# A graph block on one core: the last group's deviations by square root and reciprocal, the group in front of it written out by GpSimd

## What is computed

```python
def _layernorm(x, axis=-1, eps=1e-05):
    m = jnp.mean(x, axis=axis, keepdims=True)
    v = jnp.var(x, axis=axis, keepdims=True)
    return (x - m) / jnp.sqrt(v + eps)

# attention: per graph h = x (128x128), four score kinds, adj picks one of them
e_k = leaky_relu(einsum('bid,bjd->bij', h * a_k[:, 0], h))
alpha = softmax(where(adj == k + 1, e_k, ...))          # NEG_INF elsewhere
x = _layernorm(x + einsum('bij,bjd->bid', alpha, h))
# relational convolution, one relation for each value of adj, per direction
vals = (h[:, :, None, :] + b) * sigmoid(g[:, :, None, :] + bg)   # h = x W^T, g = h Wg^T
out = relu(sum over directions of einsum('bnmr,bmrd->bnd', onehot, vals))
x = _layernorm(x + out)
```

## Time and profile before

| | before |
|---|---|
| time, median of 3 runs | 107.75 us (107.31 to 108.19) |
| time of the profiled execution | 107.57 us |
| its span, first to last instruction | 105.8 us |
| TensorE busy | 97.1 us (92%), granted clock 0.994 |
| VectorE busy | 93.5 us (88%) |
| ScalarE busy | 89.3 us (84%) |
| GpSimd busy | 76.3 us (72%) |
| share of 16 DMA engines of the queue with all loads and stores | 52.5% |

### The profile page before, as it was taken

The page is one execution under the profiler, slowest core; times in us unless marked ns, Lnnn a source line. Parts: engine busy times, 40 slices in busy tenths (PEclk is TensorE's granted clock), DMA queues, the critical chain, the costliest instruction groups (busy, mean ns, idle before and its releaser), DMA issues.

```text
span 105.8 us, 2755 instructions
## 1 busy us (share of the span) xinstructions
PE 97.1 (92%) x682; PEld 88.6 (84%) x682; DVE 93.5 (88%) x375; ACT 89.3 (84%) x224; POOL 76.3 (72%) x139
## 2 busy tenths in 40 slices
PE   6998969999999999999999999999999998999700
PEld 6975948999999999999999999999999997888400
DVE  0169999989999999899999999999999989789970
ACT  5149998989998898999999998996999868896750
POOL 5015787598627979996989997989998981757660
PEclk9999999999999999999999999999999999999997
DMA  1999999997416258499990303011203030330355
GB/s 43 329 364 371 367 351 371 347 348 240 152 53 223 81 133 266 107 300 296 320 257 18 99 3 95 10 49 50 82 20 99 6 105 0 99 99 0 99 149 158
DMA packets 22530, 17.36 MB, mean 164 GB/s; under 512 B 1265, under 2 KB 18418, under 8 KB 22514
## 3 DMA queue, kind: packets, MB, share of 16 engines
q1 hardware_dynamic: 22370, 17.18, 52.5%
q10 hardware_dynamic: 144, 0.00, 0.1%
HBM read 12.98 MB, written 4.19 MB: 162 GB/s over the span
## 4 chain that ended last, share of the span: by engine, by line
PE 76%; SPq 6%; DMA 5%; issue 4%; DVE 4%; ACT 2%; POOL 1%; DVEq 0%
PE p_hg L1252 25%; PE p_o L1223 13%; PE p_ag L1272 12%; PE p_e L1193 9%; PE p_yt L1239 6%; PE p_ut L1212 5%; DMA inputs<-adj_rows 5%; PE p_e L1196 3%; SPq L712 2%; SPq L713 2%; DVE res L1063 1%; ACT absent L900 1%; DVE vals L1093 1%; POOL late_rs L882 1%; SPq L719 1%
## 5 line engine op out<-in xcount | busy, mean ns | idle before, releaser
L1252 PE MATMUL p_hg<-w_both,y_t 128*128 128x256 f32 x128 | 30.5, 380 | 0.0
L1252 PEld LDWEIGHTS p_hg<-w_both,y_t 128*128 128x128 f32 x128 | 23.1, 190 | 2.7 <-ACT y_t L989 0.2
L934 ACT ACTIVATE prob<-nscore,nmax 128x128 f32<-128x128 f32 x64 | 20.3, 395 | 1.2 <-DVE nmax L1048 1.2
L854 POOL TENSOR_TENSOR rs<-rs,minus_half 128x8 f32<-128x8 f32 x12 | 20.2, 1681 | 0.0
L1063 DVE SCALAR_TENSOR_TENSOR res<-p_o,rz,inputs 128x128 f32<-128x128 f32 x64 | 18.0, 345 | 0.8 <-DVE rz L1055 0.3
L1223 PE MATMUL p_o<-inputs,prob_t 128*128 128x129 f32 x128 | 17.0, 275 | 0.0
L1223 PEld LDWEIGHTS p_o<-inputs,prob_t 128*128 128x128 f32 x128 | 16.0, 191 | 0.6 <-issue 0.2
L1272 PE MATMUL p_ag<-vals,mask 128*128 128x128 f32 x116 | 15.9, 278 | 0.4 <-DVE vals L1093 0.3
L1272 PEld LDWEIGHTS p_ag<-vals,mask 128*128 128x128 f32 x116 | 14.3, 191 | 1.1 <-issue 1.0
L998 ACT ACTIVATE th<-p_hg 128x256 f32<-128x256 f32 x32 | 11.6, 379 | 3.8 <-PE p_hg L1252 3.7
L1193 PE MATMUL p_e<-inputs,xat 128*128 128x128 f32 x104 | 14.0, 278 | 0.0
(11 more groups left out here) (101 smaller groups left out, 176.6 us busy)
## 6 DMA issues: line engine op xcount, KB each, us to landing
inputs<-x_t SPq DMA_DIRECT2D x16, 256.0 KB, 5.3
inputs<-adj_rows SPq DMA_DIRECT2D x16, 256.0 KB, 5.6
inputs<-x SPq DMA_DIRECT2D x16, 256.0 KB, 6.0
out<-out_s SPq DMA_DIRECT2D x14, 256.0 KB, 2.3
out<-xat SPq DMA_DIRECT2D x4, 128.0 KB, 2.1
w_rows<-w SPq DMA_DIRECT2D x1, 128.0 KB, 3.4
wg_s<-wg_t SPq DMA_DIRECT2D x1, 128.0 KB, 3.6
w_rows<-w SPq DMA_DIRECT2D x1, 64.0 KB, 5.1
```

Source lines behind the costliest of these rows:

```text
L854: nc.gpsimd.tensor_tensor(rs[:, k, 1], rs[:, k, 0], minus_half[:], ALU.pow).then_inc(rstd1_done, 1)
L934: nc.scalar.activation(prob[:, k, i], nscore[:, k, i], ACT.Exp, scale=-1.0, bias=nmax[:, k, i:i + 1]).then_inc(exp_done, 1)
L1252: last = nc.tensor.matmul(p_hg[:, 2 * h + i], y_t[:, g % 2, part(g, h)][:, i], w_both[:], start=True, stop=True)
```

## The change

The last group's reciprocal deviations no longer come from GpSimd. ScalarE takes the square root of the variance plus epsilon (new stages std_h0:15 and std_h1:15, into last_std), and VectorE takes the reciprocal (rstd_h0:15, rstd_h1:15, into late_rs). ScalarE's square root needs another function table: a stage load_roots:15 runs a dummy square root so that the table is loaded there, and a dummy exponential behind ScalarE's last stage loads the old table again. Group 14's four outputs, by VectorE and ScalarE before, are all written by GpSimd (finish_p_h0:14, finish_p_h1:14, one instruction a graph), which also makes the negated means (late_minus). Its two half stores wait for GpSimd's semaphore alone. Columns of epsilon (eps_col) are set by one more memset at the start.

```diff
@@ -38,7 +38,7 @@
-OUT_BY = ["pppp"] * 10 + ["vvss"] * 3 + ["ssss"] + ["vsvs", "vsvv"]
+OUT_BY = ["pppp"] * 10 + ["vvss"] * 3 + ["ssss"] + ["pppp", "vsvv"]
...
@@ -65,7 +65,7 @@
-        tanhs_h0:15 tanhs_h1:15 finish_s:13 finish_s_h0:14 finish_s_h1:14 finish_s_h0:15
+        tanhs_h0:15 tanhs_h1:15 load_roots:15 finish_s:13 std_h0:15 std_h1:15 finish_s_h0:15
...
@@ -725,9 +737,12 @@
                 sp.dma_start(wg_s[:, FWD:], wg_t[FWD:].rearrange("k f e -> f k e")).then_inc(others_loaded, 16)
 
             def store_half(g, h):
-                for by, made_by in (("v", out_by_v), ("s", out_by_s)):
-                    if by in OUT_BY[g][half(h)]:
-                        sp.wait_ge(made_by, out_made(by, g - 1) + OUT_BY[g][0:2 * h + 2].count(by))
+                if g == SPLIT[0]:
+                    sp.wait_ge(late_out_by_p, 2 * h + 2)
+                else:
+                    for by, made_by in (("v", out_by_v), ("s", out_by_s)):
+                        if by in OUT_BY[g][half(h)]:
+                            sp.wait_ge(made_by, out_made(by, g - 1) + OUT_BY[g][0:2 * h + 2].count(by))
                 sp.dma_start(out_v[:, graphs(g)][:, half(h)], late_out(g)[:, half(h)]).then_inc(stored[g % 2], 16)
 
             def store(g):
...
@@ -754,6 +769,7 @@
+            nc.gpsimd.memset(eps_col[:], EPS).then_inc(const_done, 1)
...
@@ -878,12 +894,23 @@
                 pool.wait_ge(st2_done, START[g] // 2 + h + 1)
                 nc.gpsimd.tensor_scalar(late_rs[:, k, 0, half(h)], late_st[:, k, half(h), 2], 1.0 / P, EPS, ALU.mult, ALU.add)\
                     .then_inc(var2_done, 1)
+                nc.gpsimd.tensor_scalar(late_minus[:, half(h)], late_st[:, k, half(h), 1], -1.0, None, ALU.mult)\
+                    .then_inc(late_minus_done, 1)
                 pool.wait_ge(var2_done, normed_half(g, h))
                 nc.gpsimd.tensor_tensor(late_rs[:, k, 1, half(h)], late_rs[:, k, 0, half(h)], minus_half[:, half(h)],
                                         ALU.pow).then_inc(rstd2_done, 1)
 
+            def finish_p_half(g, h):
+                k = late(g)
+                pool.wait_ge(rstd2_done, normed_half(g, h))
+                pool.wait_ge(late_minus_done, h + 1)
+                for i in range(2 * h, 2 * h + 2):
+                    nc.gpsimd.tensor_scalar(late_out(g)[:, i], late_res(g)[:, i], late_minus[:, i:i + 1],
+                                            late_rs[:, k, 1, i:i + 1], ALU.add, ALU.mult).then_inc(late_out_by_p, 1)
+
             run("gpsimd", {"weigh_p": weigh, "prepare_w": prepare_w, "norm1": norm1, "y_p": y_p, "norm2": norm2, "norm2_h0": lambda g: norm2_half(g, 0),
                            "norm2_h1": lambda g: norm2_half(g, 1),
+                           "finish_p_h0": lambda g: finish_p_half(g, 0), "finish_p_h1": lambda g: finish_p_half(g, 1),
                            "norms": both_norms, "finish_p": finish_p})
             general_pool(pool)
 
...
@@ -964,17 +991,25 @@
                     nc.scalar.activation(out_s[:, k, i], res2[:, k, i], ACT.Identity, scale=rs2[:, k, 1, i:i + 1],
                                          bias=shift2[:, k, i:i + 1]).then_inc(out_by_s, 1)
 
+            def load_roots(g):
+                act.wait_ge(const_done, 8)
+                nc.scalar.activation(table_loader[:], ones_col[:], ACT.Sqrt).then_inc(roots_loaded, 1)
+
+            def std_half(g, h):
+                act.wait_ge(st2_done, START[g] // 2 + h + 1)
+                nc.scalar.activation(last_std[:, half(h)], late_st[:, late(g), half(h), 2], ACT.Sqrt, scale=1.0 / P,
+                                     bias=eps_col[:]).then_inc(last_std_done, 1)
+
             def finish_s_half(g, h):
-                k, shifts = late(g), out_made("s", g) - out_made("s", SPLIT[0] - 1)
-                if h == 0 and "s" in OUT_BY[g][half(1)]:
-                    shifts -= 1
-                act.wait_ge(late_shift_done, shifts)
-                act.wait_ge(rstd2_done, normed_half(g, h))
+                k = late(g)
+                act.wait_ge(late_shift_done, OUT_BY[g][0:2 * h + 2].count("s"))
+                act.wait_ge(last_rstd_done, h + 1)
                 act.wait_ge(r2_done, summed(g, h))
                 for i in range(2 * h, 2 * h + 2):
                     if OUT_BY[g][i] == "s":
-                        nc.scalar.activation(late_out(g)[:, i], late_res(g)[:, i], ACT.Identity, scale=late_rs[:, k, 1, i:i + 1],
-                                             bias=late_shift[:, k, i:i + 1]).then_inc(out_by_s, 1)
+                        nc.scalar.activation(late_out(g)[:, i], late_res(g)[:, i], ACT.Identity,
+                                             scale=late_rs[:, k, 1, i:i + 1], bias=late_shift[:, k, i:i + 1])\
+                            .then_inc(out_by_s, 1)
 
             def evac_weights(g):
                 act.wait_ge(w_pe, 1)
...
@@ -1006,8 +1041,10 @@
-                           "finish_s_h1": lambda g: finish_s_half(g, 1),
+                           "finish_s_h1": lambda g: finish_s_half(g, 1), "load_roots": load_roots,
+                           "std_h0": lambda g: std_half(g, 0), "std_h1": lambda g: std_half(g, 1),
+            nc.scalar.activation(table_loader[:], minus_half[:, 0:1], ACT.Exp).then_inc(table_restored, 1)
...
@@ -1112,9 +1149,13 @@
                 nc.vector.scalar_tensor_tensor(out=late_res(g)[:, half(h)], in0=sums_bank(g, h), scalar=0.0,
                                                in1=y[:, g % 4, half(h)], op0=ALU.max, op1=ALU.add).then_inc(r2_done, 1)
 
+            def rstd_half(g, h):
+                dve.wait_ge(last_std_done, h + 1)
+                nc.vector.reciprocal(late_rs[:, late(g), 1, half(h)], last_std[:, half(h)]).then_inc(last_rstd_done, 1)
+
             def finish_half(g, h):
                 k = late(g)
-                dve.wait_ge(rstd2_done, normed_half(g, h))
+                dve.wait_ge(last_rstd_done, h + 1)
                 dve.wait_ge(st2_done, START[g] // 2 + h + 1)
                 for i in range(2 * h, 2 * h + 2):
                     if OUT_BY[g][i] == "s":
```

More of the change, by code:

```diff
@@ L82 @@
         stats2:13 values_h1:14 residual2_h0:14 stats2_h0:14 finish_v:12 residual2_h1:14 values_h0:15 stats2_h1:14
-        values_h1:15 residual2_h0:15 stats2_h0:15 residual2_h1:15 finish_v_h0:14 stats2_h1:15 finish_v_h1:14
-        finish_v_h0:15 finish_v_h1:15
+        values_h1:15 residual2_h0:15 stats2_h0:15 residual2_h1:15 stats2_h1:15 rstd_h0:15 finish_v_h0:15 rstd_h1:15 finish_v_h1:15
         """,
@@ L90 @@
         finish_p:7 norms:12 finish_p:8 norms:13 finish_p:9 norms:14 norms:15 norm2:12 norm2:13 norm2_h0:14 norm2_h1:14
-        norm2_h0:15 norm2_h1:15
+        finish_p_h0:14 finish_p_h1:14
         """,
@@ L181, in program @@
         late_rs = sb("late_rs", [P, 2, 2, G])
+        last_std = sb("last_std", [P, G])
+        late_minus = sb("late_minus", [P, G])
+        eps_col = sb("eps_col", [P, 1])
         late_shift = sb("late_shift", [P, 2, G])
@@ L238, in program @@
         late_shift_done = sem("late_shift_done")
+        late_out_by_p = sem("late_out_by_p")
+        late_minus_done = sem("late_minus_done")
+        roots_loaded = sem("roots_loaded")
+        last_std_done = sem("last_std_done")
+        last_rstd_done = sem("last_rstd_done")
+        table_restored = sem("table_restored")
         tanh_done = [sem(f"tanh_done{h}") for h in range(2)]
@@ L574, in groups_of @@
             by = stage[-1]
+            if stage[:-3] in ("norm2", "finish_p"):
+                return SPLIT[:1]
+            if stage == "load_roots" or stage[:-3] in ("std", "rstd", "finish_v"):
+                return SPLIT[1:]
             if stage[:-3] == "finish_s":
@@ L1160, in _ @@
                            "stats2_h0": lambda g: stats2_half(g, 0), "stats2_h1": lambda g: stats2_half(g, 1),
+                           "rstd_h0": lambda g: rstd_half(g, 0), "rstd_h1": lambda g: rstd_half(g, 1),
                            "finish_v_h0": lambda g: finish_half(g, 0), "finish_v_h1": lambda g: finish_half(g, 1)})
```

## The result

The changed kernel takes 108.73 us (median of 8 runs, 108.48 to 109.35) against 107.34 us of the kernel before in the same comparison (8 runs, 107.26 to 108.19). The ratio is 1.0103, with a 95% interval of 1.0071 to 1.0134: slower by about 1.1 us by the ratio (the two medians lie 1.39 us apart; the next paragraphs say why). Forecast was 108.2 in 107.6 to 109.0, so the time lies in the range and the sign is right, but the loss is twice the +0.55 of the sum.

The account below looks back on a forecast made before the run. TensorE was busy 92%, but the end was taken as set by the in-order sync queue behind late store 13: +0.55 us gives 108.12 from 107.57 or 108.30 from the 107.75 median; forecast 108.2 us, range 107.6 to 109.0.

Parts of the forecast that it names:

- The load in front of group 13: ScalarE, after the last tanh: load 1.28 us and dummy 0.20 make group 13 1.50 us late, store 13 issued at 101.84.
- That rival (0.13): ScalarE's mid-stream table switch costs more than the load, about 1.28 us again for emptying and refilling: 109.5 us; chance 0.13.
- The path of the deviations: Group 15: ScalarE roots from 101.82, 0.28 us each, then VectorE reciprocals and outputs to 103.44; covered by 0.28 us.
- the +0.2 of the prediction: Group 15's deviation chain, ending at 103.44, would set the end if store 13 were not in the way: +0.2 us.
- Group 14 on GpSimd: GpSimd's four outputs of 0.45 us: halves ready at 101.05 and 101.94, queue wants them at 102.31 and 102.78; no cost.
- The queue behind store 13: Sync queue: five stores back to back from 101.84, last issue at 103.72, landing 2.02 later, end at 105.74 by issue rate.
- Four more steps of 0.47: Sync queue, four half stores behind store 13: issues 0.47 us apart put the last issue at 103.72.
- the 0.11 that I had put on top of the issue sum: Kernel's end: landing taken at 105.85, between the issue sum of 105.74 and the slower data sum of 106.04.
- The stall: Sync queue: the unexplained 0.4 us wait before the issue at 102.34 comes again in the packed queue: 108.6; chance 0.12.

## Why the prediction came out as it did

The path was right: group 13's store, late by the load, holds a queue that works in order. The loss was half of what came, and that the time itself lies in the range is in part luck of the base: the forecast set out from 107.57 and 107.75 for the kernel before, where the comparison has 107.34. From there the same +0.55 gives 107.9, and the range moved with it ends at about 108.7, where the result is.

- *The load in front of group 13* was right to a hundredth: load 1.28, dummy 0.20, group 13 done at M+3.43 (M+3.42 by the sum), store 13 at M+3.46 (M+3.44). No drain shows. The Trainium skill (ScalarE: Activation LUTs, "What ACT_TABLE_LOAD costs") has 1283 ns and a drain of some 1380 ns for every switch; here, in mid-stream, the load starts 0.02 us behind the tanh's end and the dummy 0.01 behind the load's, and the second load starts 0.02 behind its output. Its 1283 ns agree, its drain isn't there, and the measurement decides. That rival (0.13) is out.
- *The path of the deviations*: roots at M+3.34 to M+3.81 (forecast M+3.37 to M+3.84), each 0.279 us (0.28 was taken). The Trainium skill (ScalarE: Activation LUTs, "What ACT_TABLE_LOAD costs") gives about 280 ns for an activation with a bias column, and 0.83 for each element of a row, and the trace agrees. VectorE's last output ends at M+5.00 (M+5.04), ready for the queue as forecast. Behind a store 13 that isn't late this path would have cost 0.53 us (the experiment with the load moved) and not the +0.2 of the prediction, most of it the hole's 0.42.
- *Group 14 on GpSimd*: halves ready at M+2.63 and M+3.49 (M+2.65 and M+3.54), before the queue wanted them.
- *The queue behind store 13* is the step that failed, and it is a term that was mis-sized, not a wrong mechanism. "Four more steps of 0.47", 1.88 us, measured 2.38: 0.42, 0.54, 0.98 and 0.44 from issue to issue. The hole, 0.42, stands in the 0.98; the other three lie within 0.07 of the 0.47. The landing came 2.15 us after the last issue instead of 2.02. Together 0.63, and 0.02 for store 13, less the 0.11 that I had put on top of the issue sum: the landing is 0.54 late against the forecast, and +0.55 became +1.08.
- *The stall* was seen and named as a rival with a chance of 0.12 and 0.4 us. That was the misjudgment: it was in the trace of before, nothing in the change took its cause away, and "I can't name the reason" was no reason to expect it gone. The size was right. What could be had from the trace was its place: it stands behind the same place of the sync engine's list, the 79th instruction, in both kernels. A wait that no engine explains should have been carried into the sum.
- *What was covered before and isn't now*: in the kernel before, most of the hole was paid from the time until VectorE's last output. With the list moved on the last issue there is 0.11 us earlier, the landing 0.31 and the end not at all, since the second runner holds it; in the changed kernel the end is 0.38 earlier. The prediction didn't have the second runner. It did no harm there: at 2.62 us behind VectorE's last output, M+7.62, it is well ahead of the changed kernel's M+8.46.

## To carry to other kernels

When an in-order queue feeds the end, ask of every instruction that is moved which of its transfers stand ahead of the last ones: 1.5 us of table load and dummy in front of one group's outputs was passed on to the four stores behind it. A kernel's end is often the later of several runners within some tenths of a microsecond; speeding one up pays only to the next, so trace each to the end before pricing a gain. A hole in the trace that nobody explains belongs in the sum until something removes it.

## What was unexpected of the hardware

- The sync engine stands still for 0.42 us at a fixed place of its list: between a fulfilled wait and the transfer behind it, at M+3.53 in the kernel before, M+4.99 in the changed one, M+4.58 with the load moved. Five more instructions ahead of it move it to where the queue is idle (0.38 us of the end). A packet of 8 KB on an instruction queue follows the place by 1.04 to 1.50 us in all twelve traces; that the loading of instructions is the reason isn't shown.
- Issuing a transfer takes 0.37 us on a resting queue and 0.40 to 0.50 on one that is packed, and single ones 0.88 and 0.99 at M+2.63, both with a packet of 16 KB on an instruction queue in front of them; the last remain open.
- A table switch in mid-stream costs the 1.28 us of its load and 0.02 to 0.03 around it.
- The first eight products take between 1.13 and 2.01 us in different executions, by the moment at which TensorE goes from 0.21 us for a matmul to 0.11, and that moves everything behind by up to 0.9 us (M from 98.18 to 99.11). That the change has a share in how often the start is late isn't shown: 4 of 8 of its runs are late, and of the kernel before 11 of 28 in one comparison and 17 of 22 in another, told by the mean clock.
